# Two chained cross-attention layers on one core: the start of the kernel reordered, x rounded on another engine

## The chip, the cores and the metric

One Trainium2 chip, one core. The time is the device time of one execution in microseconds (us), and the number that counts is the median of the runs. Per core there are TensorE (PE, with its weight loads shown as PEld), VectorE (DVE), ScalarE (ACT), GpSimd (POOL), and SyncE (SP), which here only issues DMAs. The engines run independently and wait for one another through semaphores.

## The reference, cut to what matters

Two sequences of 2048 rows of 512 channels attend to 77 context rows each: first a single-head layer, then one with 16 heads.

```python
# layer 0 (one head, width 512)
q = x @ Wq.T + bq;  k = ctx @ Wk.T + bk;  v = ctx @ Wv.T + bv
s = where(mask == 0, -1e9, q @ k.T)
x = softmax(s) @ v + x
# layer 1 (16 heads, width 32 each)
Q = x @ W1q.T + b1q;  K = ctx @ W1k.T + b1k;  V = ctx @ W1v.T + b1v
o = concat_heads(softmax(Q @ K.T / sqrt(32)) @ V) @ W1o.T + b1o
y = o + x;  out = (y - mean(y)) / sqrt(var(y) + 1e-5) * gamma + beta
```

## The kernel before, in words

**Folded weights.** The layer-0 scores come from a folded matrix `a0` (W0q applied to the keys `k0T`) and an offset `c0`. Layer 0's output is never formed. Its values are folded instead: `u` = v0 @ W1q.T (function `fold`, one for each of the 2 batch entries) is added into the layer-1 queries, and `v0_a`/`v0_b` = v0 + b1o is added into the output.

**Split precision.** Operands of the large products are split into a rounded part and a remainder (`x_h`/`x_l`, `wq_h`/`wq_l`, `wo_h`/`wo_l`, `ct_h`/`ct_l`, `u` and `v0`). Each product takes three matmuls per 128 channels. The 77-row parts of `u`, `v0` and of layer 0's probabilities `p0` are stacked with their remainders by small DMAs inside the on-chip memory (`stack_weights`, `stack_probs`, both through `move`, L267), so that they need two matmuls instead of three. A query group is then 14 matmuls: 8 with `x_h`, 4 with `x_l`, and 2 with the stacks `u` and `p0`.

**Units.** The 4096 rows are 8 blocks of 512. A block has 4 units (`g` = 0 to 3), one for each group of 4 heads, so 32 units in all (`k` = 0 to 31). Unit k on TensorE: scores of unit k (64 small matmuls), and then, interleaved by hand, four transpose groups of the probabilities of unit k-1, the 14 query matmuls of unit k+1, a part of the output product of the block before (56 matmuls per block), and `context` of unit k-1. In g=0 `layer0` of the next block follows, and in g=3 `transpose0` of its probabilities. In units 0 to 3 there is no earlier block, so no output product.

**The other engines in a unit.** DVE takes four row maxima (`largest`), ACT four groups of exponentials (`exps`), DVE four sums and reciprocals (`inverse_sums`), and POOL scales (`scale_probs`). ACT empties each transpose group (`leave_pt`), rounds the context result (`round_ct`), and writes `q` (`round_q`). ACT also rounds the next block's x, two chunks in a unit with g=1 and two with g=2 (`round_x`, L450). POOL forms the remainder (`x_rest`, L323). Every engine works strictly in the order written. There are 8 PSUM banks, bank 0 for the queries, 1 to 4 scores, 5 transposes (`ps_t`), 6 context (`ps_pv`), 7 output (`ps_out`).

**The start.** SP queues these loads in order: ctx, w0k and w0q in halves, x of block 0, w0v, w1q, then w1k, w1v and w1o into buffers as they come free. ACT's own queue loads the column biases, the mask, `bo_sb` and `rows_sb`; the last two are one row of HBM broadcast to 128 partitions. TensorE does k0T, a0, c0, v0T, layer0 of block 0, k1T, the v0 rows (`to_rows`), transpose0, fold(0), 12 query matmuls, half of v1T, the last 2 query matmuls, the other half of v1T, and enters unit 0. `fold(1)` is in unit 1. DVE does layer 0's softmax first and forms `wq_l` (L656) after it.

Of the kernel before, what the change touches and what calls it, by code (L numbers as in the profile page):

```python
# [5 lines left out]
F32 = mybir.dt.float32  # L6
# [10 lines left out]
P = 128  # L17
# [22 lines left out]
STEPS = UNITS + 2  # L40
LAST = BLOCKS - 1


def xattn_kernel(nc, xT, x, mask, ctxT, w0k, w0q, w0v, w1q, w1k, w1v, w1o, cols, rows, out):
# [7 lines left out]
    with ExitStack() as ctx:  # L52
# [7 lines left out]
        with ExitStack() as prep:  # L60
# [22 lines left out]

        wq_h = sb("wq_h", [P, CH, DIM], F32R)
# [137 lines left out]
        def _(sp):  # L222
# [7 lines left out]
            sp.dma_start(raw2[:], w1q.rearrange("(c p) e -> p c e", p=P)).then_inc(ld_w1q, 16)  # L230
            sp.wait_ge(mm_k0T, 2)
# [3 lines left out]
            sp.wait_ge(mm_v0T, 2)  # L235
            sp.dma_start(raw3[:], w1o.rearrange("(c p) e -> p c e", p=P)).then_inc(ld_w1o, 16)
# [80 lines left out]
        def _(pool):  # L317
# [80 lines left out]
            pool.wait_ge(ld_rows, 16)  # L398
# [29 lines left out]
        def _(act):  # L428
            act.dma_start(cols_sb[:].rearrange("p a c -> p (a c)"), cols).then_inc(ld_cols, 16)
            act.dma_start(mask_sb[:].rearrange("p t k -> p (t k)"), mask[0, 0]).then_inc(ld_mask, 16)  # L430
            flat = rows.rearrange("(o n) -> o n", o=1)
            act.dma_start(bo_sb[:], flat[:, 2 * DIM:3 * DIM].to_broadcast([P, DIM])).then_inc(ld_bo, 16)
            act.dma_start(rows_sb[:].rearrange("p a d -> p (a d)"),
                          flat[:, 0:2 * DIM].to_broadcast([P, 2 * DIM])).then_inc(ld_rows, 16)
# [8 lines left out]
            def round_x(i, b, first, last):  # L443

                if not block_exists(i, b):
                    return
                wait(act, ld_xT, 16 * (blocks(i, b) + 1))
                wait(act, q_done, CH * blocks(i, b - 1))
                for c in range(first, last):
                    nc.scalar.activation(x_h[:, b % 2, c], x_raw[:, c], ACT.Copy).then_inc(xh_ready, 1)  # L450
# [28 lines left out]
            act.wait_ge(bk1_ready, 1)  # L479
            leave(bank[1:3], mm_k1T, k1T, bk1_scaled, k1T_ready, scale=SCALE)  # L480
# [9 lines left out]
            leave(bank[5:7], mm_v1T, v1T, cols_sb[:, 5], v1T_ready, first=2, last=CH)  # L490
# [31 lines left out]
            def step(i, k):  # L522
# [624 lines left out]
```

## Time and profile before

| | before |
|---|---|
| median of 3 runs | 425.58 us (423.49 to 426.01) |
| profiled execution: time / span of the core | 424.65 us / 422.9 us |
| PE busy | 392.4 us (93%) |
| ACT busy | 278.4 us (66%) |
| DVE busy | 276.3 us (65%) |
| POOL busy | 225.3 us (53%) |
| chain that ended last | PE 78%, DMA 7%, ACT 6% of the span |
| mean granted TensorE clock | 0.985 |

The span runs from the first to the last instruction. The profiled execution lies 0.93 us below the median and 1.75 us above its own span. A share of 93% is a mean over a start, a long middle part and an end, which have different limits, so the stages have to be read one by one.

### The profile page before, as it was taken

What the parts mean: (1) busy time and instruction counts of PE and PEld (TensorE: products, weight loads), DVE (VectorE), ACT (ScalarE), POOL (GpSimd) and SP (SyncE); (2) the same over time, 40 slices, a digit from 0 to 9 for tenths busy, and PEclk for the clock granted to TensorE, in tenths of its full rate; (3) what the DMA queues carried; (4) which work ended last, traced back from release to release, by engine and by line L of the source; (5) the groups of instructions that cost most, each with busy time, mean ns of one, the idle gap of its engine ahead of it and who ended that gap; (6) DMA issues with size and microseconds to landing.
All of it is one profiled execution on the core that took longest, in us unless ns stands there. A gap on an engine that the chain in (4) does not pass through costs nothing.

```text
span 422.9 us, 12177 instructions
## 1 busy us (share of the span) xinstructions
PE 392.4 (93%) x4968; PEld 297.5 (70%) x4968; DVE 276.3 (65%) x675; ACT 278.4 (66%) x811; POOL 225.3 (53%) x249
## 2 busy tenths in 40 slices
PE   2999988799999999999999999999999999899990
PEld 2996755577777777787777776878777776677570
DVE  0145466558766887678766876697678876557656
ACT  0433778677768865896688667877688658756720
POOL 0400357234437754785477553775377637812866
PEclk9999999899999999999999999999999999899997
DMA  8993103300024300521042204230243002240012
GB/s 254 399 327 125 48 2 131 131 16 4 1 57 167 116 11 19 184 97 52 1 170 84 95 2 138 86 126 2 72 150 127 2 21 81 81 151 2 34 66 99
DMA packets 19230, 39.44 MB, mean 93 GB/s; under 512 B 1865, under 2 KB 5449, under 8 KB 18151
## 3 DMA queue, kind: packets, MB, share of 16 engines
q1 hardware_dynamic: 18599, 37.72, 25.9%
q10 hardware_dynamic: 576, 0.96, 0.8%
q8 instruction: 39, 0.64, 0.6%
q14 instruction: 16, 0.13, 0.1%
HBM read 26.49 MB, written 8.39 MB: 82 GB/s over the span
## 4 chain that ended last, share of the span: by engine, by line
PE 78%; DMA 7%; ACT 6%; SPq 2%; POOL 2%; DVE 2%; issue 1%; POOLq 0%
PE ps_q L912 20%; PE ps_out L977 19%; PE ps_t L937 12%; PE ps_s L926 7%; PE ps_pv L952 7%; DMA p_b<-p_l 5%; PE ps_out L873 4%; PE ps_s L849 3%; ACT prob L497 2%; SPq L267 2%; DMA raw<-in_w0k 2%; ACT pt L506 1%; PE ps_pv L886 1%; PE ps_pv L849 1%; PE ps_s L994 1%
## 5 line engine op out<-in xcount | busy, mean ns | idle before, releaser
L344 POOL TENSOR_TENSOR prob<-prob,rc 128x308 f32<-128x308 f32 x128 | 91.1, 718 | 156.5 <-DVE rc L691 156.0
L497 ACT ACTIVATE prob<-ps_s,mx 128x77 f32<-128x77 f32 x512 | 120.7, 327 | 0.7 <-DVE mx L682 0.7
L506 ACT ACTIVATE pt<-ps_t 77x512 f32<-77x512 f32 x128 | 76.2, 595 | 53.1 <-PE ps_t L937 52.5
L689 DVE TENSOR_REDUCE sm<-prob 128x4 f32<-128x308 f32 x128 | 59.4, 464 | 37.8 <-ACT prob L497 37.7
L937 PE MATMUL ps_t<-ident,prob 128*77 128x128 f32 x512 | 79.7, 279 | 3.3 <-ACT pt L506 3.3
L682 DVE TENSOR_REDUCE mx<-ps_s 128x4 f32<-128x308 f32 x128 | 54.8, 471 | 36.9 <-PE ps_s L926 36.9
L937 PEld LDWEIGHTS ps_t<-ident,prob 128*77 128x77 f32 x512 | 62.1, 148 | 21.8 <-issue 5.5
L912 PE MATMUL ps_q<-x_h,wq_h 128*128 128x512 f32 x128 | 54.8, 428 | 0.0
L912 PE MATMUL ps_q<-x_h,wq_l 128*128 128x512 f32 x128 | 54.0, 422 | 0.0
L323 POOL TENSOR_TENSOR x_l<-x_raw,x_h 128x512 fp32r<-128x512 f32 x32 | 41.1, 1287 | 21.2 <-ACT x_h L450 21.2
L926 PEld LDWEIGHTS ps_s<-k1T,q 32*64 32x64 f32 x2048 | 25.9, 131 | 28.9 <-issue 16.4
L977 PE MATMUL ps_out<-wo_h,ct_h 128*128 128x512 f32 x112 | 44.9, 401 | 0.0
L977 PE MATMUL ps_out<-wo_h,ct_l 128*128 128x512 f32 x112 | 44.7, 399 | 0.0
L977 PE MATMUL ps_out<-wo_l,ct_h 128*128 128x512 f32 x112 | 44.7, 399 | 0.0
L512 ACT ACTIVATE ct_h<-ps_pv 128x512 fp32r<-128x512 f32 x32 | 19.2, 599 | 38.6 <-PE ps_pv L952 38.5
L912 PE MATMUL ps_q<-x_l,wq_h 128*128 128x512 f32 x128 | 42.2, 413 | 0.0
L360 POOL TENSOR_TENSOR y<-y,rows_sb 128x512 f32<-128x512 f32 x28 | 36.0, 1285 | 8.7 <-ACT y L519 8.7
L362 POOL TENSOR_TENSOR y<-y,rows_sb 128x512 f32<-128x512 f32 x28 | 36.0, 1287 | 2.2
L952 PE MATMUL ps_pv<-pt,v 77*32 77x512 f32 x256 | 34.1, 602 | 1.1 <-ACT pt L506 1.0
L926 PE MATMUL ps_s<-k1T,q 32*64 32x77 f32 x2048 | 31.3, 240 | 2.9 <-ACT q L468 1.8
L912 PEld LDWEIGHTS ps_q<-x_h,wq_h 128*128 128x128 f32 x128 | 25.1, 196 | 3.4 <-issue 0.3
L912 PEld LDWEIGHTS ps_q<-x_h,wq_l 128*128 128x128 f32 x128 | 24.8, 194 | 3.4 <-issue 0.2
(115 smaller groups left out, 603.4 us busy)
## 6 DMA issues: line engine op xcount, KB each, us to landing
x_raw<-in_xT SPq DMA_DIRECT2D x8, 1024.0 KB, 6.5
y<-in_x SPq DMA_DIRECT2D x28, 256.0 KB, 2.7
out<-y SPq DMA_DIRECT2D x28, 256.0 KB, 2.0
p_b<-p_a SPq DMA_DIRECT2D x8, 154.0 KB
mask_sb<-in_mask SPq DMA_DIRECT2D x7, 154.0 KB, 5.4
raw<-in_w0k SPq DMA_DIRECT2D x2, 512.0 KB, 7.5
raw<-in_w0q SPq DMA_DIRECT2D x2, 512.0 KB, 10.0
raw<-in_w0v SPq DMA_DIRECT2D x1, 1024.0 KB, 12.3
```

Source lines behind the costliest of these rows:

```text
L323: nc.gpsimd.tensor_tensor(x_l[:, b % 2, c], x_raw[:, c], f32(x_h[:, b % 2, c]), ALU.subtract).then_inc(xl_ready, 1)
L344: nc.gpsimd.tensor_tensor(ap, ap, wide(rc[:, k % 2, h], KEYS), ALU.mult).then_inc(prob_done, 1)
L360: nc.gpsimd.tensor_tensor(y[:, t], y[:, t], rows_sb[:, 0], ALU.mult).then_inc(gamma_done, 1)
L497: e = nc.scalar.activation(prob[:, k % 2, h, t], ps_s[:, h, t * KEYS:(t + 1) * KEYS], ACT.Exp, bias=mx[:, k % 2, h, t:t + 1])
L506: nc.scalar.activation(pt[:, h], ps_t[0:KEYS, :], ACT.Copy).then_inc(pt_ready, 1)
L682: nc.vector.reduce_max(mx[:, k % 2, h], ps_s[:, h, 0:TILES * KEYS].rearrange("p (t k) -> p t k", k=KEYS), AX_X, negate=True).then_inc(max_ ...
L689: nc.vector.reduce_sum(sm[:, k % 2, h], prob[:, k % 2, h], AX_X).then_inc(sum_done, 1)
L912: mm = nc.tensor.matmul(ps_q[:], w, v, start=(m == 0), stop=(m == QUERY - 1))
L926: mm = nc.tensor.matmul(ps_s[r:r + P // 2, h, t * KEYS:(t + 1) * KEYS], q[rows_of, k % 2, t * P + r:t * P + r + P // 2], k1T[rows_of, g, b ...
L937: mm = nc.tensor.transpose(ps_t[0:KEYS, t * P:(t + 1) * P], prob[:, k % 2, h, t], ident[:])
L952: mm = nc.tensor.matmul(ps_pv[rows_of, :], v1[:, b % 2, own], pt[:, h], start=True, stop=True)
L977: mm = nc.tensor.matmul(ps_out[:], w, v, start=(m == 0), stop=(m == OUTPUT - 1))
```

## The change

It does eight things.

1. Eighteen identity transposes (`WARM`) run on TensorE as soon as the identity exists, before the first load has landed.
2. ACT's queue keeps only the column biases. The mask moves to SP's queue behind w1q. `bo_sb` and `rows_sb` move to SP's queue behind the stacks, w1o and the x of block 1.
3. The w1o load moves behind the stacks of `p0` and `u` of the first batch entry.
4. ACT rounds w1q before it empties v0T. DVE forms `wq_l` before layer 0's softmax.
5. TensorE's start has layer0 before v0T, then 6 query matmuls, transpose0, fold(0), 6 more, k1T, and the last 2. v1T moves to unit 0, behind the scores, and its rows to that unit's end. wo is rounded by ACT in unit 0.
6. fold(1) moves from unit 1 to unit 2.
7. The value rows of layer 0 are made in unit 3 through `ps_out`, one batch entry at a time. TensorE waits for DVE to have read the first before it writes the second. Their stacks are SP's last step before its loop. The x load of block 2 goes in front of the `p0` stacks of block 1.
8. From block 1 on, x is rounded on DVE, behind the third sum of the units with g=1 and g=2. In g=1 ACT's exponentials and transposes follow the order of the other units.

```diff
             sp.dma_start(raw2[:], w1q.rearrange("(c p) e -> p c e", p=P)).then_inc(ld_w1q, 16)
+            sp.dma_start(mask_sb[:].rearrange("p t k -> p (t k)"), mask[0, 0]).then_inc(ld_mask, 16)
             sp.wait_ge(mm_k0T, 2)
             sp.dma_start(raw0[:], w1k.rearrange("(c p) e -> p c e", p=P)).then_inc(ld_w1k, 16)
             sp.wait_ge(mm_a0, 2)
             sp.dma_start(raw1[:], w1v.rearrange("(c p) e -> p c e", p=P)).then_inc(ld_w1v, 16)
-            sp.wait_ge(mm_v0T, 2)
-            sp.dma_start(raw3[:], w1o.rearrange("(c p) e -> p c e", p=P)).then_inc(ld_w1o, 16)
...
-            next_inputs(0, 0)
             stack_probs(0, 0)
             stack_weights(u_a, u_b, slice(0, 1), u_stacked[0], u_h_ready, u_ready, 1)
-            stack_weights(v0_a, v0_b, slice(0, BATCH), v0_stacked, v0_h_ready, v0_ready, BATCH)
-
+            sp.dma_start(raw3[:], w1o.rearrange("(c p) e -> p c e", p=P)).then_inc(ld_w1o, 16)
+            next_inputs(0, 0)
+            flat = rows.rearrange("(o n) -> o n", o=1)
+            sp.dma_start(bo_sb[:], flat[:, 2 * DIM:3 * DIM].to_broadcast([P, DIM])).then_inc(ld_bo, 16)
+            sp.dma_start(rows_sb[:].rearrange("p a d -> p (a d)"),
+                         flat[:, 0:2 * DIM].to_broadcast([P, 2 * DIM])).then_inc(ld_rows, 16)
             stack_weights(u_a, u_b, slice(1, 2), u_stacked[1], u_h_ready, u_ready, 2)
             sp.wait_ge(mm_u, BATCH)
             sp.wait_ge(wq_ready, CH)
             for t in range(TILES):
                 load_rows(0, 0, t)
+            next_inputs(0, 1)
             stack_probs(0, 1)
-            next_inputs(0, 1)
+            stack_weights(v0_a, v0_b, slice(0, BATCH), v0_stacked, v0_h_ready, v0_ready, BATCH)
...
@@ -427,11 +432,6 @@
         @block.scalar
         def _(act):
             act.dma_start(cols_sb[:].rearrange("p a c -> p (a c)"), cols).then_inc(ld_cols, 16)
-            act.dma_start(mask_sb[:].rearrange("p t k -> p (t k)"), mask[0, 0]).then_inc(ld_mask, 16)
-            flat = rows.rearrange("(o n) -> o n", o=1)
-            act.dma_start(bo_sb[:], flat[:, 2 * DIM:3 * DIM].to_broadcast([P, DIM])).then_inc(ld_bo, 16)
-            act.dma_start(rows_sb[:].rearrange("p a d -> p (a d)"),
-                          flat[:, 0:2 * DIM].to_broadcast([P, 2 * DIM])).then_inc(ld_rows, 16)
...
             act.wait_ge(ld_cols, 16)
             leave(bank[1:3], mm_k0T, k0T, cols_sb[:, 1], k0T_ready)
-            round_x(0, 0, 0, CH)
-            leave(bank[5:7], mm_v0T, v0T, cols_sb[:, 2], v0T_ready)
-            exp0(0, 0)
+            round_first_x()
             act.wait_ge(ld_w1q, 16)
             for c in range(CH):
                 nc.scalar.activation(wq_h[:, c], raw2[:, c], ACT.Copy).then_inc(wq_h_ready, 1)
-            act.wait_ge(bk1_ready, 1)
-            leave(bank[1:3], mm_k1T, k1T, bk1_scaled, k1T_ready, scale=SCALE)
+            leave(bank[5:7], mm_v0T, v0T, cols_sb[:, 2], v0T_ready, first=0, last=2)
+            exp0(0, 0)
+            leave(bank[5:7], mm_v0T, v0T, cols_sb[:, 2], v0T_ready, first=2, last=CH)
             round_p0(0, 0)
             def round_u(b):
                 act.wait_ge(mm_u, b + 1)
                 nc.scalar.activation(u_a[0:KEYS, b], bank[5 + 2 * b][0:KEYS, :], ACT.Copy).then_inc(u_h_ready, 1)
+            def round_wo(first, last):
+                act.wait_ge(ld_w1o, 16)
+                for c in range(first, last):
+                    nc.scalar.activation(wo_h[:, c], raw3[:, c], ACT.Copy).then_inc(wo_h_ready, 1)
+
             round_u(0)
-            leave(bank[5:7], mm_v1T, v1T, cols_sb[:, 5], v1T_ready, first=0, last=2)
+            act.wait_ge(bk1_ready, 1)
+            leave(bank[1:3], mm_k1T, k1T, bk1_scaled, k1T_ready, scale=SCALE)
             round_q(0, 0)
...
                 exps(i, k, 1)
+                if k == 0:
+                    leave(bank[5:7], mm_v1T, v1T, cols_sb[:, 5], v1T_ready, first=0, last=2)
+                leave_pt(i, k - 1, 2)
+                exps(i, k, 2)
+                if k == 0:
+                    leave(bank[5:7], mm_v1T, v1T, cols_sb[:, 5], v1T_ready, first=2, last=CH)
+                if g == 3:
+                    normalise(i, b - 1, 0)
+                leave_pt(i, k - 1, 3)
...
-                    round_x(i, b + 1, 0, 1)
-                    exps(i, k, 3)
-                    leave_pt(i, k - 1, 2)
-                    round_x(i, b + 1, 1, 2)
-                    leave_pt(i, k - 1, 3)
                     exp0(i, b + 1)
-                else:
-                    leave_pt(i, k - 1, 2)
-                    exps(i, k, 2)
...
+                    normalise(i, b - 2, 2)
+                if k == 0:
+                    round_wo(0, 3)
+                if k == 2:
                     round_u(1)
                 round_q(i, k + 1)
                 if g == 0:
                     normalise(i, b - 2, 3)
-                if type(i) is int and k == 0:
-                    act.wait_ge(ld_w1o, 16)
-                    for c in range(CH):
-                        nc.scalar.activation(wo_h[:, c], raw3[:, c], ACT.Copy).then_inc(wo_h_ready, 1)
+                if k == 0:
+                    for v in range(BATCH):
+                        act.wait_ge(mm_v1, v + 1)
+                        nc.scalar.activation(v1[:, v], bank[5 + v][0:KEYS, :], ACT.Copy).then_inc(v1_ready, 1)
+                    round_wo(3, CH)
...
         def _(dve):
+            def round_x(i, b, first, last):
+
+                if not block_exists(i, b):
+                    return
+                wait(dve, ld_xT, 16 * (blocks(i, b) + 1))
+                wait(dve, q_done, CH * blocks(i, b - 1))
+                for c in range(first, last):
+                    nc.vector.tensor_copy(x_h[:, b % 2, c], x_raw[:, c]).then_inc(xh_ready, 1)
+
...
             dve.wait_ge(c0_ready, 1)
+            def wq_rest(c):
+                dve.wait_ge(wq_h_ready, c + 1)
+                nc.vector.tensor_tensor(wq_l[:, c], raw2[:, c], f32(wq_h[:, c]), ALU.subtract).then_inc(wq_ready, 1)
+
+            for c in range(CH):
+                wq_rest(c)
             layer0_leave(0, 0)
             layer0_mask(0, 0)
             layer0_select(0, 0)
             layer0_shift(0, 0)
             layer0_probs(0, 0)
...
             def u_rest(b):
                 dve.wait_ge(u_h_ready, b + 1)
-                if b == 1:
-                    dve.wait_ge(v0_stacked, 48)
                 nc.vector.tensor_tensor(rest[:, b], bank[5 + 2 * b][0:KEYS, :], f32(u_a[0:KEYS, b]), ALU.subtract).then_inc(u_ready, 1)
             p0_rest(0, 0)
             u_rest(0)
-            dve.wait_ge(ld_bo, 16)
-            for b in range(BATCH):
-                dve.wait_ge(mm_v0, b + 1)
-                nc.vector.tensor_tensor(v0o[:, b], bank[3 + b][0:KEYS, :], bo_sb[0:KEYS], ALU.add).then_inc(v0o_ready, 1)
-            for v in range(BATCH):
+
+            def v0_leave(v):
+                dve.wait_ge(ld_bo, 16)
+                dve.wait_ge(mm_v0, v + 1)
+                nc.vector.tensor_tensor(v0o[:, v], ps_out[0:KEYS, :], bo_sb[0:KEYS], ALU.add).then_inc(v0o_ready, 1)
                 dve.wait_ge(v0o_ready, v + 1)
                 nc.vector.tensor_copy(v0_a[0:KEYS, v], v0o[:, v]).then_inc(v0_h_ready, 1)
...
                 inverse_sums(i, k, 2)
+                if g == 1:
+                    round_x(i, b + 1, 0, 2)
                 if g == 2:
+                    round_x(i, b + 1, 2, CH)
                     variance(i, b - 1, 0)
+                if k == 3:
+                    v0_leave(0)
                 inverse_sums(i, k, 3)
-                if type(i) is int and k == 1:
+                if k == 2:
                     u_rest(1)
+                if k == 3:
+                    v0_leave(1)
+                    v0_rest(0)
+                    v0_rest(1)
...
+            pe.wait_ge(ident_ready, 1)
+            for _ in range(WARM):
+                nc.tensor.transpose(ps_out[:, 0:P], ident[:], ident[:])
             pe.wait_ge(ld_ctx, 16)
             project(bank[1:3], raw0, ctxT_sb, mm_k0T, ld_w0k)
             pe.wait_ge(k0T_ready, CH)
@@ -1023,15 +1040,10 @@
             for c in range(CH):
                 mm = nc.tensor.matmul(ps_out[:, 0:BATCH * KEYS], bq0_wide[:, c], k0T[:, c], start=(c == 0), stop=(c == CH - 1))
             mm.then_inc(mm_c0, 1)
-            project(bank[5:7], raw3, ctxT_sb, mm_v0T, [ld_w0v, ld_w0v])
             pe.wait_ge(a0_ready, 2)
             pe.wait_ge(c0_ready, 1)
             layer0(0, 0)
-            project(bank[1:3], raw0, ctxT_sb, mm_k1T, [ld_w1k, ld_w1k])
-            pe.wait_ge(v0T_ready, CH)
-            pe.wait_ge(ident_ready, 1)
...
+            pe.wait_ge(wq_ready, 3)
+            query(0, 0, 0, 6)
+            pe.wait_ge(ident_ready, 1)
+            pe.wait_ge(v0T_ready, CH)
             transpose0(0, 0)
             fold(0, 0, CH)
             pe.wait_ge(wq_ready, CH)
-            query(0, 0, 0, 3 * CH)
-            pe.wait_ge(u_ready, 1)
-            pe.wait_ge(p0l_ready, 1)
-            project(bank[5:7], raw1, ctxT_sb, mm_v1T, [ld_w1v, ld_w1v], 0, 2)
-            pe.wait_ge(u_stacked[0], 48)
+            query(0, 0, 6, 3 * CH)
+            project(bank[1:3], raw0, ctxT_sb, mm_k1T, [ld_w1k, ld_w1k])
             query(0, 0, 3 * CH, QUERY)
-            project(bank[5:7], raw1, ctxT_sb, mm_v1T, [ld_w1v, ld_w1v], 2, CH)
             pe.wait_ge(k1T_ready, CH)
-            pe.wait_ge(v0o_ready, BATCH)
             def step(i, k):
                 g, b = k % CH, k // CH
...
                     pe.wait_ge(wo_ready, CH)
                 scores(i, k)
-                if type(i) is int and k == 0:
-                    pe.wait_ge(v1T_ready, CH)
-                    to_rows(bank[5:7], v1T, mm_v1)
-                if type(i) is int and k == 1:
+                if k == 0:
+                    pe.wait_ge(u_ready, 1)
+                    pe.wait_ge(p0l_ready, 1)
+                    project(bank[5:7], raw1, ctxT_sb, mm_v1T, [ld_w1v, ld_w1v])
+                if k == 1:
                     pe.wait_ge(v1_ready, BATCH)
...
                 query(i, k + 1, 0, 5)
                 transposes(i, k - 1, 1)
-                if type(i) is int and k == 1:
+                if k == 2:
                     pe.wait_ge(add0_done, 2)
                     fold(1, 0, 2)
+                if k == 3:
+                    pe.wait_ge(u_ready, 2)
+                    to_rows(ps_out, v0T, 0, mm_v0)
...
                     query(i, k + 1, 5, 10)
                 transposes(i, k - 1, 3)
-                if type(i) is int and k == 1:
+                if k == 0:
+                    pe.wait_ge(v1T_ready, CH)
+                    for v in range(BATCH):
+                        to_rows(bank[5 + v], v1T, v, mm_v1)
+                if k == 2:
                     fold(1, 2, CH)
+                if k == 3:
+                    pe.wait_ge(v0o_ready, 1)
+                    to_rows(ps_out, v0T, 1, mm_v0)
                 if g == 0:
                     layer0(i, b + 1)
```

## Rows read from the trace of the kernel before

**Rows 1.** Windows of units 0 to 3 and block 3: length, PE, PEld, DVE, ACT, POOL busy, PEclk, DMA, GB/s

```profile
43.77:51.22 7.45, 7.45 (x222) 6.34 (x225) 4.15 (x12) 6.69 (x24) 2.85 (x5) 1.00 0.15 49
51.22:64.19 12.97, 10.99 (x118) 6.43 (x121) 7.59 (x21) 9.42 (x28) 8.19 (x9) 1.00 0.01 2
64.19:73.19 9.00, 7.32 (x104) 5.13 (x103) 5.90 (x15) 7.93 (x25) 6.15 (x7) 1.00 0.46 153
73.19:85.03 11.84, 9.68 (x114) 6.70 (x116) 5.44 (x14) 7.39 (x23) 3.89 (x6) 0.86 0.37 127
129.31:174.07 44.76, 44.59 (x605) 33.55 (x606) 33.89 (x83) 33.31 (x98) 28.01 (x32) 1.00 0.25 83
```

**Rows 2.** Chain that ended last, to 90 us: start, us, what held it

```profile
1.24 6.43 DMA raw<-in_w0k
...
7.80 5.86 PE ps_s L849 x32
...
14.40 4.47 PE ps_s L849 x32
...
19.92 2.10 PE ps_t L849 x16
...
24.12 2.27 PE ps_out L873 x128
...
32.11 3.45 PE ps_t L1039 x8
...
37.77 3.11 DMA u_b<-rest
...
57.91 0.52 ACT x_h L450
...
65.67 1.16 PE ps_q L912 x5
...
69.30 0.84 ACT prob L497 x4
...
79.16 4.09 DMA p_b<-p_l
```

**Rows 3.** DMA queues from 5 to 9 us: packets, MB, share of 16 engines

```profile
q10 hardware_dynamic: 267, 0.74, 62.5%
q1 hardware_dynamic: 405, 0.40, 30.0%
```

**Rows 4.** DMA queue of SP from 4 to 5 us

```profile
q1 hardware_dynamic: 369, 0.38, 107.2%
```

**Rows 5.** The page's DMA issues: KB each, median us to landing

```profile
raw<-in_w1q SPq DMA_DIRECT2D x1, 1024.0 KB, 13.6
```

**Rows 6.** Timeline of the start: start, duration, engine, line, operation, idle before

```profile
7.47 2.05 SPq L230 DMA_DIRECT2D raw<-in_w1q  x1
...
26.54 0.48 DVE L587 TENSOR_TENSOR m<-ps_out,c 128x308 f32<-128x308 f32 x1 [6.26 <-PE ps_out L873]
...
26.93 0.31 DVE L596 TENSOR_SCALAR n<-mask_sb 128x308 f32<-128x308 int32 x1
...
29.76 2.17 ACT L478 ACTIVATE wq_h<-raw 128x512 fp32r<-128x512 f32 x4
...
30.61 0.48 DVE L630 TENSOR_TENSOR m<-m,stat 128x308 f32<-128x308 f32 x1
...
31.01 2.49 DVE L656 TENSOR_TENSOR wq_l<-raw,wq_h 128x512 fp32r<-128x512 f32 x4
...
38.01 0.75 DVE L671 CAST v_a<-v0o 77x512 fp32r<-77x512 f32 x2
```

**Rows 7.** Timeline of DVE in block 3, from 138 to 176 us

```profile
141.93 0.90 DVE L596 TENSOR_SCALAR n<-mask_sb 128x308 f32<-128x308 int32 x1
...
163.61 0.86 DVE L682 TENSOR_REDUCE mx<-ps_s 128x4 f32<-128x308 f32 x2 [1.19 <-PE ps_s L926]
```

**Rows 8.** Waits of PEld, 85 to 400 us: total us, times, longest

```profile
PEld ps_q L912 <- DMA p_b<-p_l: 2.4, 5, 0.5
```

More of the change, by code:

```diff
@@ L40 @@
 STEPS = UNITS + 2
+WARM = 18
 LAST = BLOCKS - 1
@@ L64, in xattn_kernel @@
             v1T = sb("v1T", [P, CH, BATCH * KEYS], F32, prep)
-            rest = sb("rest", [KEYS, BATCH, DIM], F32R, prep)
+            k0T = sb("k0T", [P, CH, BATCH * KEYS], F32, prep)
+            bq0_wide = sb("bq0_wide", [P, CH, P], F32, prep)
             v0T = sb("v0T", [P, CH, BATCH * KEYS], F32, prep)
             v0o = sb("v0o", [KEYS, BATCH, DIM], F32, prep)
-            k0T = sb("k0T", [P, CH, BATCH * KEYS], F32, prep)
             raw0 = sb("raw0", [P, CH, DIM], F32, prep)
-            bq0_wide = sb("bq0_wide", [P, CH, P], F32, prep)
-            bo_sb = sb("bo_sb", [P, DIM], F32, prep)
             before_y = 4 * CH * BLOCK + KC * BLOCK + 2 * TILES * GCOLS
-            taken = 3 * CH * DIM + 2 * BATCH * DIM + 4 * CH * BATCH * KEYS + CH * P + DIM
+            taken = 3 * CH * DIM + BATCH * DIM + 4 * CH * BATCH * KEYS + CH * P
             sb("unused", [P, before_y - taken], F32, prep)
@@ L81, in xattn_kernel @@
         y = sb("y", [P, TILES, DIM])
+        rest = sb("rest", [KEYS, BATCH, DIM], F32R)
+        bo_sb = sb("bo_sb", [P, DIM])
         wq_h = sb("wq_h", [P, CH, DIM], F32R)
@@ L441, in leave, with round_first_x @@
                     nc.scalar.activation(to[:, c], src, ACT.Identity, bias=bias[:, c:c + 1], scale=scale).then_inc(ready, 1)
[L443 to L450, printed above, removed]
+            def round_first_x():
+                act.wait_ge(ld_xT, 16)
+                for c in range(CH):
+                    nc.scalar.activation(x_h[:, 0, c], x_raw[:, c], ACT.Copy).then_inc(xh_ready, 1)
             def exp0(i, b):
@@ L648, in _ @@
             dve.wait_ge(c0_ready, 1)
+            def wq_rest(c):
+                dve.wait_ge(wq_h_ready, c + 1)
+                nc.vector.tensor_tensor(wq_l[:, c], raw2[:, c], f32(wq_h[:, c]), ALU.subtract).then_inc(wq_ready, 1)
+            for c in range(CH):
+                wq_rest(c)
             layer0_leave(0, 0)
@@ L653, in _ @@
             layer0_probs(0, 0)
-            for c in range(CH):
-                dve.wait_ge(wq_h_ready, c + 1)
-                nc.vector.tensor_tensor(wq_l[:, c], raw2[:, c], f32(wq_h[:, c]), ALU.subtract).then_inc(wq_ready, 1)
             def u_rest(b):
                 dve.wait_ge(u_h_ready, b + 1)
-                if b == 1:
-                    dve.wait_ge(v0_stacked, 48)
                 nc.vector.tensor_tensor(rest[:, b], bank[5 + 2 * b][0:KEYS, :], f32(u_a[0:KEYS, b]), ALU.subtract).then_inc(u_ready, 1)
@@ L853, in project, with to_rows @@
                         mm.then_inc(made, 1)
-            def to_rows(banks, src, made):
-                for b in range(BATCH):
-                    for e in range(CH):
-                        mm = nc.tensor.transpose(banks[b][0:KEYS, e * P:(e + 1) * P],
-                                                 src[:, e, b * KEYS:(b + 1) * KEYS], ident[:])
-                    mm.then_inc(made, 1)
+            def to_rows(to, src, b, made):
+                for e in range(CH):
+                    mm = nc.tensor.transpose(to[0:KEYS, e * P:(e + 1) * P], src[:, e, b * KEYS:(b + 1) * KEYS], ident[:])
+                mm.then_inc(made, 1)
             def layer0(i, b):
@@ L910, in query @@
                             wait(pe, p0_stacked, 48 * (blocks(i, b) + 1))
+                            if b < BATCH:
+                                wait(pe, u_stacked[b], 48)
                         w, v = ((u_a[:, b % 2, own], p0_a[:, b % 2]), (u_b[:, b % 2, own], p0_b[:, b % 2]))[m - 3 * CH]
@@ L1029, in _ @@
             layer0(0, 0)
-            project(bank[1:3], raw0, ctxT_sb, mm_k1T, [ld_w1k, ld_w1k])
-            pe.wait_ge(v0T_ready, CH)
-            pe.wait_ge(ident_ready, 1)
-            to_rows(bank[3:5], v0T, mm_v0)
-            pe.wait_ge(ld_w1q, 16)
+            project(bank[5:7], raw3, ctxT_sb, mm_v0T, [ld_w0v, ld_w0v])
             def fold(b, first, last):
@@ L1063, in part @@
                         output(i, b - 1, OUT_AT[g][n], OUT_AT[g][n + 1])
-                if type(i) is int and k == CH - 1:
-                    pe.wait_ge(u_stacked[1], 48)
                 if type(i) is int and k == CH + 1:
```

34 lines of the change are left out of this document (10 added, 24 removed).

## Prediction

> **What bounds the kernel now.** I read the windows first, then the chain of work that ended last, then the queues and the timeline of the start.
>
> From unit 4 on TensorE is the bound: block 3 holds 44.59 us of PE work in 44.76 us [rows 1]. The change takes no matmul out of these blocks, so what it can win is won before unit 4, which starts at 85.03. In units 0 to 3 there is no output product, and PE is busy for 7.45 of 7.45, 10.99 of 12.97, 7.32 of 9.00 and 9.68 of 11.84 us [rows 1]: unit 0 is PE's, units 1 and 2 are mostly ACT's, and unit 3 has waits and a clock of 0.86.
>
> Up to unit 0 the chain runs through the loads and then through PE almost without a break. PE starts at 7.80, when the first half of w0k lands (1.24 + 6.43 = 7.67) [rows 2]. The reader should see two things there. The first 32 projection matmuls take 5.86 us and the same 32 of a0 take 4.47, a difference of 1.4 us although the granted clock is shown as full in both: the first ones run slower. And from 5 to 9 us the two broadcast loads of ACT's queue move 0.74 MB while SP's queue, with everything that the start needs, moves 0.40 MB [rows 3]; in the microsecond before, it moved 0.38 MB by itself [rows 4].
>
> **Part 1, the loads come earlier.** SP's queue could have moved 4 x 0.38 = 1.52 MB in those 4 us and moved 0.40 [rows 3, 4]; the missing 1.12 MB are 2.9 us. The mask's 0.16 MB add 0.4 to 0.5 us, since it now queues behind w1q. I take 3.4 us. Bounds: only the 0.74 MB of bytes, 1.9 us; and 5.5 MB (ctx and five loads) at 0.38 from 2.2 us on, which puts w1q at 16.7, 4.4 us earlier. w1q landed at 7.47 + 13.6 = 21.1 [rows 5, 6], and now lands at 17.7. For w0k, nearer to the front, ctx and half of w0k (0.83 MB) end near 5.0 instead of 7.7. bo_sb and rows_sb come after the x of block 1 and land, an estimate, near 45 us; their first readers are in units 3 and 5.
>
> **Part 2, eighteen transposes in front.** They start near 1.5 us. The projection's 4.47 / 32 = 0.14 us [rows 2] prices them at 2.5 us, a slow rate of twice that at 5.0, so they end between 4.0 and 6.5 against w0k at 5.0. I take a start of k0T at 5.4 and leave open whether k0T takes 4.5 or 5.9. The Trainium skill, TensorE: Matmul & The Clock Gate, Part 4, says that transposes do not count as busy for the clock gate; by that k0T would still take 5.9, otherwise 4.5. No row here shows transposes alone in front of matmuls. Part 3 shows that the whole 1.4 us hardly matter, since another chain ends later.
>
> **Part 3, up to unit 0.** PE: k0T from 5.4 to 9.9 or 11.3; its second half is emptied in 0.7; a0 and c0 take 19.92 - 14.40 = 5.5 [rows 2], to 16.1 or 17.5; 0.5 for the copy of c0; layer0 2.27, to 18.9 or 20.3; v0T 2 x 2.10, to 23.1 or 24.5; six query matmuls at 0.23 [rows 2], to 24.5 or 25.9. The other chain: w1q at 17.7, ACT's first rounding chunk (2.17 / 4) to 18.3, DVE's `wq_l` 2.49 to 20.8, and only behind it layer 0's softmax, which took from 26.54 to 31.09 [rows 6], so 4.55, to 25.4. The moved `wq_l` is thus on the path; it was hidden behind the softmax. Both meet at transpose0 near 25.4: 0.45 for it, fold(0) 3.45 [rows 2], six query matmuls 1.4, k1T 4.2, the last two 0.5, to 35.4. The stacks of `u` took from 35.56 to 40.88 behind the fold, 5.3 us [rows 2]; now from 29.3 to 34.6, hidden by k1T's end at 34.9. w1o is queued behind them, so they meet no big load. Then ACT empties k1T and writes q, and scores start at 36.5, against 43.77 [rows 1]: **7.3 us earlier.**
>
> **Part 4, units 0 to 3.**
> - Unit 0 takes over v1T, 4.2, on an engine that has no idle time there: 7.45 + 4.2 = 11.65. Its rows were in the unit before, and ACT's extra pieces (v1T 1.3, wo 2.2 and v1 1.2) add to 4.0 of exponentials and q, under PE's sum.
> - Unit 1 loses fold(1), 3.45, and two roundings on ACT. It then resembles unit 2 of before: 9.00 less 2 x 0.52 for x [rows 1, 2], plus 0.45 for exp0 and handovers: 8.7, against 12.97.
> - Unit 2 takes the fold: 7.32 + 3.45 = 10.8 of PE work less overlaps: 10.6, against 9.00.
> - Unit 3 gains the v0 rows, 0.9, and a wait. PE may not write the second half of `ps_out` until DVE has added b_o to the first, and DVE's add is queued behind the third sum, which waits for the third exponentials (0.85 a group [rows 2]), near 8.5 us into the unit; the add ends at 9.2. PE is through its other work at 7.4 and stands, with the last six query matmuls, context and the next scores queued behind. From 9.2: rows 0.4, two matmuls, then the `p0` stacks. They landed 10.1 us into the unit before (79.16 + 4.09 [rows 2]); now 2.3 MB of y rows, x and mask stand in front of them, 6 us at 0.38 from about 3 us on, so 9.5 to 10.5. Then 0.5, context 1.0. That is 11.8, and I add 0.7 for a lower clock behind the stand: 12.5, against 11.84. Its bounds are 11.3 and 15.
> - The v0 stacks are ready to be issued near 1 us into unit 4 and are wanted at its end, 9 us later: nothing.
>
> Sum: 11.65 + 8.7 + 10.6 + 12.5 = 43.45 against 41.26, **2.2 us longer.**
>
> **Part 5, from unit 4 on.** ACT loses four roundings of x in a block; PE waits for none of them, so nothing is won. DVE gains four copies. The nearest row is the cast of `v_a`, 0.375 each with POOL idle [rows 6], so 1.5 us in a block on an engine with 33.9 of 44.8 us busy [rows 1]. In g=2 two copies stand ahead of the next unit's maxima, where DVE waited 1.19 us for PE [rows 7]; 0.75 fits. The same kind of operation, L596, took 0.31 us with POOL idle and 0.90 in block 3 with POOL at work [rows 6, 7]. That fits the Trainium skill, SBUF — State Buffer, section Who interferes with whom, by which a copy or a tensor_scalar in a two-port mode and a GpSimd operation exclude each other for a whole instruction. In g=2, though, POOL waits for the very copy, so I price this part at nothing and keep the other case as a rival. `largest` feeds exp, then `round_p0`, then the stacks, for which PE already waits up to 0.5 us [rows 8]: that chain has no slack of its own.
>
> **Sum.** -7.3 + 2.2 = -5.1. On the profiled execution's own 424.65 us that is 419.6; from the median of 425.58, which is 0.9 above it, 420.5. I predict 420.0. One per cent, 4.3 us, is about what a measurement of this kernel tells from no change, so faster begins below 421.3 and slower above 429.8.
>
> **Rivals.**
> 1. *Less is won.* The loads shift by 1.9 instead of 3.4 (+1.5), unit 3's stand and the stacks behind 2.3 MB cost 2 us more, or the clock falls for longer there (the 0.86 row). For it: three chains meet in unit 3 and I laid them out without gaps. Against it: the rate in rows 3 and 4. 420.0 + 3.5 = 423.5. Chance 0.30.
> 2. *More is won.* w1q lands at 16.7, so PE's own chain sets transpose0 at 24.5 (-0.9), and unit 3 runs at 11.3 (-1.2), since its exponentials start earlier without ACT's roundings: 417.9. Chance 0.13.
> 3. *Slower: the copies queue behind POOL in every block.* Place: g=2, in front of `largest` of g=3, where the `p0` stack chain starts. If each copy takes 0.375 plus a POOL operation of 1.3, two take 3.3, less the 1.19 of slack: 2.1 us in each of six blocks, 12.7 in all, so 432.7. At 1.0 us a copy the loss is 0.8 a block and the gain of 5.1 is gone; at 1.8 us a copy it passes 429.8. For it: L596's growth. Against it: POOL's order, and rows 1 leave DVE 10 us a block. Chance 0.10.
> 4. *The change doesn't do what it says:* SP's queue stays slow without the broadcasts (HBM or the small packets, not ACT's queue, set the rate of rows 3). Then w1q lands at 21, and unit 0 starts 3.3 us later: 423.3. Chance 0.04.
>
> **How the numbers follow.** The forecast, 418.5 to 421.8, has 0.43. Range 416.5 to 425: it leaves out rival 3 and the ends of 1 and 2. Faster by over 1%: 0.8 of 0.43, 0.13, and 0.2 of 0.30: 0.55. Slower by over 1%: most of rival 3, 0.09. The rest, 0.36, is within 1%.
>
> **What the changed profile would show.** Part 1: the queue table from 5 to 9 us with SP alone near 0.38 MB/us, and w1q's landing near 17.7. Part 2: the time of the first 32 matmuls. Part 3: DVE's softmax starting when `wq_l` ends, near 20.8, and scores at 36.5. Part 4: units of 11.6, 8.7, 10.6 and 12.5, with PE standing before L859's second group of v0 rows. Part 5: PE busy over 99% of block 3 in 44.8 us, and copies near 0.4 us. I would be wrong if DVE's copies grow past 1 us, if the `p0` stacks come late in unit 3, or if TensorE's clock falls in units 1 to 3, where its gaps are.

## The result, and the profile after

The changed kernel takes 431.82 us (430.38 to 433.16) against 424.90 for the kernel before (a fourth run beside the three above): 1.0183 times as long, with a 95% interval of 1.0146 to 1.0221. The forecast was 420.0. Its profiled execution took 430.87 us, with a span of 429.0 against 422.9.

First the windows of units 0 to 4 and of block 3 in the changed kernel (length; busy time of PE, PEld, DVE, ACT, POOL; granted clock; DMA share; GB/s). They answer to [rows 1].

```profile
41.73:53.42 11.69, 11.69 (x247) 10.66 (x247) 4.15 (x12) 8.58 (x27) 4.04 (x5) 1.00 0.50 199
53.42:62.84 9.42, 7.57 (x107) 5.22 (x102) 7.66 (x18) 6.72 (x23) 3.82 (x5) 1.00 0.01 3
62.84:73.33 10.49, 10.49 (x111) 6.36 (x111) 8.25 (x22) 7.49 (x23) 9.89 (x10) 1.00 0.01 2
73.33:89.45 16.12, 10.59 (x118) 6.59 (x115) 8.59 (x20) 7.63 (x23) 4.15 (x6) 0.88 0.63 201
89.45:101.15 11.70, 10.79 (x235) 8.43 (x231) 5.32 (x14) 6.92 (x22) 2.80 (x4) 0.87 0.08 26
136.42:181.08 44.66, 44.44 (x600) 33.50 (x597) 35.10 (x87) 31.32 (x94) 28.28 (x31) 1.00 0.25 81
```

The middle is untouched: block 3 takes 44.66 us against 44.69 (129.31 to 174.00 before), with DVE 1.3 us busier and ACT 2 us less. Nearly all that is missing against the forecast lies in three places: unit 0 starts 5.2 us late, unit 3 takes 3.6 us more and unit 4 takes 2.5 us more. This table is worked out from where each unit's scores start.

| us | before | forecast | after |
|---|---|---|---|
| unit 0 starts | 43.7 | 36.5 | 41.7 |
| unit 0 | 7.5 | 11.65 | 11.7 |
| unit 1 | 13.0 | 8.7 | 9.4 |
| unit 2 | 9.1 | 10.6 | 10.5 |
| unit 3 | 11.8 | 12.5 | 16.1 |
| unit 4 | 9.2 | 9.2 | 11.7 |
| unit 5 to the end | 328.7 | 328.7 | 327.9 |

Next the chain that ended last, in the changed kernel (start, us, what held it). It answers to [rows 2].

```profile
1.24 4.71 DMA raw<-in_w0k
...
6.09 4.98 PE ps_s L863 x32
...
17.79 2.35 PE ps_out L885 x128
20.13 0.72 PE ps_t L863 x4
20.86 2.88 issue
23.74 3.03 PE ps_t L863 x12
26.77 2.58 PE ps_pv L863 x16
...
79.08 7.31 DMA p_b<-p_l
...
86.44 1.22 PE ps_q L926 x2
87.65 1.87 PE ps_pv L966 x8
89.52 1.35 PE ps_s L940 x63
```

The reader should see two stands. At 20.86 PE stops for 2.88 us in the middle of v0T, held by nothing that the profile names ("issue"). The remaining 28 matmuls then take 5.6 us, where 3.7 were due, so the whole projection takes 9.2 us instead of 4.2; the granted clock is 0.70 from 23.74 to 29.35 us. And the `p0` stacks of block 1 land 7.31 us after their last issue, where it was 4.09 [rows 2]. Behind this stand too everything is slow: the context takes 1.87 us instead of 1.0, and the granted clock of units 3 and 4 is 0.88 and 0.87.

### The profile page after: what moved, and what is told of

It reads as the page before. It is cut to its first block, busy times and chain, and to the rows that moved or that the text cites. A ratio compares the mean times of both kernels' runs of the same rounds, so it can differ in the third digit from the quotient of the medians.

```text
span 429.0 us, 12203 instructions
## 1 busy us (share of the span) xinstructions
PE 397.7 (93%) x4986; PEld 301.0 (70%) x4986; DVE 288.0 (67%) x703; ACT 265.1 (62%) x783; POOL 228.3 (53%) x249
## 4 chain that ended last, share of the span: by engine, by line
PE 79%; DMA 7%; ACT 5%; SPq 3%; issue 2%; POOL 2%; DVE 1%; POOLq 0%
PE ps_q L926 20%; PE ps_out L991 19%; PE ps_t L951 13%; PE ps_s L940 7%; PE ps_pv L966 7%; DMA p_b<-p_l 6%; PE ps_out L885 4%; PE ps_s L863 3%; SPq L267 2%; PE ps_t L863 1%; ACT prob L498 1%; DMA raw<-in_w0k 1%; PE ps_pv L863 1%; ACT pt L507 1%; PE ps_pv L898 1%
## 5 line engine op out<-in xcount | busy, mean ns | idle before, releaser
L327 POOL TENSOR_TENSOR x_l<-x_raw,x_h 128x512 fp32r<-128x512 f32 x32 | 44.5, 1396 | 23.1 <-ACT x_h L447 13.4
L926 PE MATMUL ps_q<-x_h,wq_h 128*128 128x512 f32 x128 | 53.9, 421 | 0.0
L513 ACT ACTIVATE ct_h<-ps_pv 128x512 fp32r<-128x512 f32 x32 | 19.2, 600 | 40.6 <-PE ps_pv L966 40.6
L926 PEld LDWEIGHTS ps_q<-x_h,wq_h 128*128 128x128 f32 x128 | 24.5, 191 | 3.2 <-issue 0.3
```

What stands on the lines that cost most here:

```text
L327: nc.gpsimd.tensor_tensor(x_l[:, b % 2, c], x_raw[:, c], f32(x_h[:, b % 2, c]), ALU.subtract).then_inc(xl_ready, 1)
L926: mm = nc.tensor.matmul(ps_q[:], w, v, start=(m == 0), stop=(m == QUERY - 1))
```

## The experiments

All are the changed kernel with one edit or several. Ratios are to the kernel before, taken beside it on the same chip.

**1. Stacks in front of the x load.**

```diff
-            next_inputs(0, 1)
             stack_probs(0, 1)
+            next_inputs(0, 1)
```

> The changed kernel, with the stacks of block 1's probabilities put back in front of the x and mask load of block 2 on SP's queue. In the changed kernel unit 3 lasts 16.1 us, PE stands 2.8 us for these stacks, and unit 4 lasts 11.7 us where it lasted 9.2 before. Theory A (the stacks queue behind 1.2 MB of x and mask): they land 4 to 5 us after the last of them is issued instead of 7.3, unit 3 shortens by 3 us, and unit 4 by 1 to 2 us because the clock no longer falls; in all 4 to 5 us less. Theory B (the 1 MB of y rows, which stands in front in both orders, holds them back): less than 1 us. Theory C (the wait for the first v0 rows sets unit 3): unit 3 stays above 15 us.

Measured: 427.26 us, ratio 1.0072 (1.0033 to 1.0112), against 1.0183 unedited. Unit 3 takes 11.80 us, unit 4 10.68. SP's queue in this kernel, in time order, and PE's first matmul behind the stacks, which names no wait:

```profile
74.94 1.86 SPq L252 DMA_DIRECT2D y<-in_x  x4
77.65 0.81 SPq L267 DMA_DIRECT2D p_b<-p_a  x1
78.51 0.72 SPq L267 DMA_DIRECT2D p_a<-p_l  x1
79.27 0.80 SPq L267 DMA_DIRECT2D p_b<-p_l  x1
80.18 0.56 SPq L245 DMA_DIRECT2D x_raw<-in_xT  x1
...
83.81 0.49 PE L926 MATMUL ps_q<-p_a,u_a 128*128 128x512 f32 x1
```

In the changed kernel the x load was issued at 76.56, just in front of the stacks, and this matmul ran at 86.44. Theory A holds: units 3 and 4 shorten by 16.12 + 11.70 - 11.80 - 10.68 = 5.3 us. What unit 4 still has above its 9.2 is mostly 1.07 us of "issue" inside its layer0. The start kept its stand, 2.72 us.

**2. v0T in front of layer0 again.**

```diff
+            project(bank[5:7], raw3, ctxT_sb, mm_v0T, [ld_w0v, ld_w0v])
             pe.wait_ge(a0_ready, 2)
             pe.wait_ge(c0_ready, 1)
             layer0(0, 0)
-            project(bank[5:7], raw3, ctxT_sb, mm_v0T, [ld_w0v, ld_w0v])
```

> The changed kernel, with TensorE's v0T projection back in front of layer0 of block 0. In the changed kernel PE stands 2.9 us inside v0T, 20.9 to 23.7 us, with nothing released, and then runs slowly. Theory A (layer0 runs through its 128 small matmuls in 2.3 us, faster than the instructions behind them are fetched): the stand goes or falls under 1 us, and scores of unit 0 start near 38.5 us instead of 41.7. Theory B (the stand belongs to the time, not to the order: the queues are full of loads then): a stand of 2 to 3 us is seen between 19 and 25 us whatever stands there, and scores start near 41.

Measured: 433.25 us (427.30 to 434.83). The four runs lie too far apart for a ratio, so only the rows of the start are used. The stand is gone, as theory A had it, but unit 0 starts at 41.12 all the same. The chain shows why:

```profile
17.12 2.10 PE ps_t L863 x16
19.22 2.10 PE ps_pv L863 x16
21.32 2.32 PE ps_out L885 x128
23.66 0.48 DVE m L589
...
28.37 1.11 PE ps_pv L898 x4
29.47 4.39 PE ps_t L1051 x8
```

v0T takes its 4.2 us. Layer0 ends 3.5 us later, layer 0's softmax starts 1.3 us later and is now bare: PE waits 3.2 us for it, and the fold behind that wait takes 4.39 us instead of 3.45. The order avoids one stand and uncovers another wait, so its expected 38.5 us failed.

**3. The same order, but the queue empty.**

```diff
-            sp.wait_ge(mm_k0T, 2)
+            sp.wait_ge(l0_done, 1)
             sp.dma_start(raw0[:], w1k.rearrange("(c p) e -> p c e", p=P)).then_inc(ld_w1k, 16)
-            sp.wait_ge(mm_a0, 2)
             sp.dma_start(raw1[:], w1v.rearrange("(c p) e -> p c e", p=P)).then_inc(ld_w1v, 16)
```

> The changed kernel, with w1k and w1v loaded only when layer0 of block 0 is done (near 20 us) instead of at 11 and 16 us, so that SP's queue is empty from about 20 us while PE runs into v0T. Theory B (the instruction fetch queues behind w1k and w1v): the stand of 2.9 us shrinks to under 1 us and scores of unit 0 start near 38.5 us. Theory A (the fetch is late whatever the queue holds, because layer0 uses instructions up too fast): the stand stays above 2 us. w1k would land near 25 us, before its use at 31.

Measured: 428.61 us, ratio 1.0108 (1.0064 to 1.0151). Unit 0 starts at 37.51, 4.2 us earlier, while units 3 and 4 stay long (16.03 and 12.25 us). Here TensorE's timeline of this kernel at the place of the stand:

```profile
19.05 0.79 PE L862 MATMUL ps_t<-ctxT_sb,raw 128*128 128x154 f32 x4
20.10 1.84 PE L862 MATMUL ps_t<-ctxT_sb,raw 128*128 128x154 f32 x12 [0.26 <-issue]
```

And in the changed kernel:

```profile
20.06 0.79 PE L863 MATMUL ps_t<-ctxT_sb,raw 128*128 128x154 f32 x4
23.74 0.53 PE L863 MATMUL ps_t<-ctxT_sb,raw 128*128 128x154 f32 x2 [2.88 <-issue]
```

TensorE's instructions and their order are the same in both, and only SP's loads differ: the stand falls from 2.88 to 0.26 us. The DMA table names the packets. In the changed kernel, from 21 to 22 us, beside a full load queue:

```profile
q1 hardware_dynamic: 195, 0.40, 101.4%
q8 instruction: 1, 0.02, 5.8%
```

This is the first packet on that queue (it starts at 21.5 us). With late loads it starts at 17.9 us, where the load queue is running empty, and PE stands only 0.26 us. So a fetch of instructions came 3.6 us later while w1k and w1v were moving, or 2.7 us later if one counts from the start of layer0 (17.79 and 16.77 us), and PE, which had used up the 256 instructions of layer0 in 2.35 us, ran dry. Experiments 2 and 3 together say that the stand needs both: the burst of layer0 just in front, and the loads.

That the packet is TensorE's is inferred from the times; the table doesn't say. The times agree closely, though. Nine kernels stop at this place, and in each PE goes on 2.2 to 2.7 us after the packet starts: 21.5 and 23.74 in the changed kernel, 17.9 and 20.10 here, 22.5 and 25.12 in experiment 7.

The same sign stood in the kernel before, one block later, and the prediction passed over it:

```profile
48.94 2.28 PE ps_out L873 x128
...
52.05 0.99 issue
```

Here layer0 of block 1 is followed by a stand of 0.99 us, again 2.5 us behind a packet of the kind "instruction" (50.5 and 53.04), and here the DMA engines are all but idle (share 0.02). All thirteen kernels stand there for 0.55 to 0.99 us. So behind such a burst PE can stand for up to 1 us with hardly a load in flight; at the start, with the loads, it was 2.9. That the burst is the cause of the shorter stand is inferred: no run moves that layer0 away.

**4. x rounded on ACT again** (the copies on DVE removed, `round_x` back in ACT's order).

> The changed kernel, with x rounded on ACT as in the kernel before (one chunk behind the third and one behind the fourth exponentials of the units with g=1 and g=2). If the rounding on DVE costs nothing in the middle of the kernel, as forecast, the blocks from 3 on keep their 44.5 to 45.2 us, and units 1 and 2 get up to 1 us longer each: 0 to 2 us slower in all. If the copies on DVE hold up the maxima, blocks 2 to 6 get shorter by 0.3 us or more each and the kernel is 1 to 3 us faster.

Measured: 434.05 us, ratio 1.0227 (1.0182 to 1.0273). Unit 1 takes 10.40 us instead of 9.42. From unit 5 to the start of unit 31 it takes 1.7 us more, 1.5 of it in unit 29, where nothing is rounded. (Unit 29 takes 13.68 us here and 12.16 in the changed kernel, but 13.61 in the kernel before too, at a granted clock of 0.87.) The intervals of this ratio and of the changed kernel's overlap, so a gain from DVE is not shown here; experiment 8 shows it.

**5. Edits 1 and 3 together.**

> The changed kernel with two edits at once: the stacks of block 1 in front of the x load of block 2, and w1k and w1v loaded only when layer0 of block 0 is done. Theory: the two causes are separate and add up. Unit 0 starts near 37.5 us, unit 3 takes 11.8, unit 4 starts near 81.1 and takes 9.2 to 10.7; a span near 421 us and a time near 422.5, 1 to 3 us under the kernel before and 8 to 9 us under the changed kernel. Rival: with unit 0 earlier, another transfer (the u stacks behind w1k and w1v, or the y rows) takes the place, and the sum is 2 us or more short of that.

Measured: 423.09 us, ratio 0.9968 (0.9941 to 0.9995); span 420.1. Unit 0 starts at 37.74, unit 4 takes 10.06. Against the changed kernel's 1.0183 the ratio falls by 0.0215 here, by 0.0111 in experiment 1 and by 0.0075 in experiment 3: the causes add up. Unit 3 takes 13.41 instead of 11.8, since the stacks land 6.09 us after their last issue and this wait of PE is back in part:

```profile
PE ps_q L925 <- DMA p_b<-p_l: 1.4, 1, 1.4
```

**6. The same without the eighteen transposes** (`WARM = 0`).

> The same as the run before it in this set (both edits), without the eighteen identity transposes. If they raise the clock, the first 32 projection matmuls take 5.9 us again instead of about 5.0. The scores of unit 0 should still start within 0.5 us of the other run, since the chain through w1q and layer 0's softmax ends later than PE's. 36 instructions less in front also shift where PE runs out of fetched instructions: if the 1 us stand at the end of layer0 in unit 4 belongs to the position in the instruction stream, it moves or goes.

Measured: 421.85 us, ratio 0.9957 (0.9930 to 0.9984). Two lines of its chain:

```profile
5.62 7.30 PE ps_s L862 x32
...
39.16 0.94 PE ps_s L939 x45
```

k0T takes 7.30 us, against 4.56 in experiment 5 and 5.86 in the kernel before, and unit 0 starts at 39.16, 1.4 us later than with the transposes, which is more than expected. But units 3 and 4 take 12.40 and 9.22 instead of 13.41 and 10.06, and the two kernels can't be told apart. The stand at the end of layer0 in unit 4 (0.50 us in experiment 5) is gone.

**7. Mask and broadcasts back on ACT's queue** (with edits 1 and 3).

> Both edits, with the mask and the two broadcast rows back on ACT's queue at the very start. If the broadcasts hold SP's queue back, w0k and w1q land 2 to 3 us later (w0k near 7.7, w1q near 21), and unit 0 starts 2 to 2.7 us later; the rest stays. If they don't matter, unit 0 starts within 0.5 us.

Measured: 425.88 us, ratio 1.0019 (0.9988 to 1.0051), against 0.9968 without: 2.2 us of time. From 5 to 9 us SP's queue moves 0.39 MB again, against 1.31 in experiment 5. w0k lands at 7.1 us and w1q at 21.4 (5.6 and 18.6 in experiment 5), about as expected. Unit 0 starts at 41.60, 3.9 us later, which is more than the expected 2 to 2.7: k0T takes 7.43 us though the transposes ran, and PE stood 1.6 us between them and the load. (This profiled execution took 430.33 us, above the kernel's median, so of its rows only the start is used.)

**8. Rounding on ACT** (with edits 1 and 3).

> Both edits, with x rounded on ACT as before. Expected: 1 to 2 us slower than with the rounding on DVE, nearly all of it in units 1 and 2, and nothing from unit 5 on. If the rounding on DVE costs anything in the middle, blocks 2 to 6 are shorter here.

Measured: 424.98 us, ratio 1.0022 (0.9988 to 1.0057), 2.3 us above experiment 5, with intervals that overlap only at their edges. Units 1 and 2 take 10.47 and 12.04 us instead of 9.69 and 10.47. In unit 2 the granted clock is 0.86 here and 1.00 there, so its 1.6 us are a slow stretch of the clock in this one execution, and whether the rounding brought it on isn't shown. Blocks 2 to 6 take 224.4 against 223.4 us, so they aren't shorter. Nothing was expected there; 1.2 us are unit 20, which takes 10.47 us here and 9.31 in experiment 5, but 10.48 in the changed kernel with its rounding on DVE.

**9 to 11. The y rows behind the stacks.** Edits 1 and 3, and on SP's queue:

```diff
-            sp.wait_ge(mm_u, BATCH)
-            sp.wait_ge(wq_ready, CH)
-            for t in range(TILES):
-                load_rows(0, 0, t)
             stack_probs(0, 1)
             next_inputs(0, 1)
             stack_weights(v0_a, v0_b, slice(0, BATCH), v0_stacked, v0_h_ready, v0_ready, BATCH)
+            sp.wait_ge(mm_u, BATCH)
+            sp.wait_ge(wq_ready, CH)
+            for t in range(TILES):
+                load_rows(0, 0, t)
```

> The changed kernel with both edits (stacks in front of the x load, w1k and w1v late) and the four y row loads of block 0 moved behind the stacks of block 1, the x of block 2 and the stacks of v0. With both edits alone PE still stood 1.4 us in unit 3 for the stacks, which landed 6.1 us after their last issue. Theory: the y rows (1 MB) in front of them are what is left, because fold(1) in unit 2 releases them right there. Then the stacks land 4.1 to 4.5 us after the issue, the stand goes, unit 3 takes 11.8 instead of 13.4 us, unit 4 9.3 to 10; 1.5 to 2.5 us faster. Rival: the v0 rows' own wait keeps unit 3 above 13.

> The same three edits without the eighteen identity transposes. Unit 0 starts 1.4 us later (39.1 against 37.7), as in the pair without the third edit; units 3 and 4 take 11.8 and 9.3. If the transposes are worth what unit 0 shows, this is about 1 us slower than the other; if the stand for instructions at the end of layer0 in unit 4 comes from their 36 instructions, the two are equal within 0.5 us.

> The three edits, with the transposes, and w1q queued in front of w0v. Unit 0's start hangs on w1q (landed at 18.6 us), its rounding, and layer 0's softmax behind it. With w1q 2.5 us earlier, PE's own chain (layer0 at 20, v0T to 24.4, six query matmuls) sets transpose0, near 25.8 instead of 26.5: 0.5 to 0.8 us gained, no more. If w0v then lands after 20 us and PE waits for it, nothing or a loss.

Measured: 423.67 us, ratio 1.0000 (0.9963 to 1.0037); without transposes 423.28, 0.9975 (0.9942 to 1.0008); with w1q in front 424.62, 1.0005 (0.9973 to 1.0038). Unit 3 takes 11.71 us in all three, so the y rows were what was left. But the expected 1.5 to 2.5 us were not gained: it was paid back at once. TensorE in unit 4 of the first of them:

```profile
87.02 2.34 PE L884 MATMUL ps_out<-a,x_raw 128*32 128x77 f32 x127
90.79 0.23 PE L884 MATMUL ps_out<-a,x_raw 128*32 128x77 f32 x1 [1.44 <-issue]
...
92.80 1.12 PE L950 MATMUL ps_t<-ident,prob 128*77 128x128 f32 x4
```

The y rows are now issued from 83.6 to 87.4 us, the queue is busy right under layer0 (0.33 MB from 88 to 89 us), and layer0 stands 1.44 us for its last instruction (0.50 in experiment 5). Unit 5 follows at a granted clock of 0.59 (93 to 97 us) and takes 13.74 us instead of 12.16. Without transposes unit 0 starts at 38.20 instead of 37.35, and unit 4 takes 9.26 instead of 11.00. w1q in front gives nothing: PE's own chain already set transpose0 (26.28 and 26.21 us).

## Why the prediction was wrong

**Part 1, the loads: right mechanism, size too large.** SP's queue moved 1.29 MB from 5 to 9 us, not 1.52, and w1q landed at 5.51 + 13.7 = 19.2, 1.9 us earlier, not 3.4. Experiment 7 shows that the loads on ACT's queue are the cause, and that they cost 2.2 us of time. The mask had landed at 4.6 us there, so from 5 to 9 us it was the two broadcasts.

**Part 2, the transposes: they do raise the clock.** k0T took 4.98 us behind them, and 7.30 without (experiment 6); in experiment 3 the transposes themselves speed up, from one in 0.21 us to one in 0.11. Only the estimate that this hardly matters was roughly right: they were worth 1.4 and 0.85 us in unit 0's start, and nothing that could be told in the kernel's time.

**Part 3 failed, in its step "v0T 2 x 2.10, to 23.1 or 24.5".** I took the projection from its matmuls, as if PE's instructions were always there. It took from 20.1 to 29.35: 2.9 us of stand and 2.1 us of slower matmuls (granted clock 0.70). Experiment 3 removes the stand without touching TensorE's program, and unit 0 starts at 37.5, 4.2 us earlier; 0.7 of the 1.0 us by which that misses the forecast's 36.5 is w1q's landing (18.4 against 17.7). In the kernel before, v0T's 64 instructions stood between a0 and layer0, and PE didn't stop there: its packet started at 22.9 us, before layer0 began at 24.12. I had not asked what the moved block does to the fetch. In the same move ACT's exp0 stood behind the emptying of v0T, so the softmax waited with it. Unit 0's late start is 5.2 of the 11.3 us that the profiled execution lies above the forecast for it (430.87 against 419.6).

**Part 4 failed in unit 3, in its step "so 9.5 to 10.5".** The stacks landed 13.1 us into the unit. I had named the 2.3 MB in front of them, and counted their bytes at 0.38 MB/us, but from 76 to 82 us SP's queue moved only 0.30 to 0.34, and the last stack took 7.3 us from issue to landing. Moving the x load behind them removed the stand in experiment 1 and left 1.4 us of it in experiment 5, which moving the y rows cleared in 9. The wait for the v0 rows, which I had made unit 3's limit, was there (1.2 us), and with the queue clear unit 3 took 11.7 to 11.8, my sum without the clock's share. Unit 3 is 3.6 us of the 11.3.

**A term was missing: unit 4.** I let the slower clock end with unit 3. It ran on into unit 4 (0.87), which also has layer0 and its own 0.9 us for instructions: 2.5 us. Rival 1 had the loads, the stacks and the clock at 3.5 us together; no rival had the fetch.

**Right:** units 0, 1 and 2 (11.7, 9.4, 10.5 against 11.65, 8.7, 10.6), the hidden `u` stacks, and most of Part 5. Unit 1 is the loosest: its own terms, 9.00 - 1.04 + 0.45, give 8.4 and not 8.7. DVE's copies took 0.42 us in the median and 1.35 at most; block 3 kept its length; rival 3 didn't happen. Rival 4 is refuted by the 1.29 MB. Freeing ACT was worth 2.3 us in time (experiment 8), where the forecast had counted 1.0 in unit 1. The units show 0.8 to 1.0 in unit 1 (experiments 4 and 8); the 1.6 in unit 2 of experiment 8 stand beside a lower clock, so where the rest comes from is open.

**Two more sums were off, without effect on the outcome.** In rival 3 the time passes 429.8 from 1.4 us a copy on, not from 1.8: 2 x 1.4 less 1.19, in six blocks, is 9.7. And 0.8 of 0.43, 0.13 and 0.2 of 0.30 make 0.53, not 0.55.

**Open:** why the clock's share differs from run to run; why the packet came late in the changed kernel and in experiments 1 and 4, but in time in the kernel before and in experiment 2, where the load queue was as full when it came (102.9% and 104.4% of the engines in that microsecond); and what sets the length of the stand in unit 4. Its place goes with the 36 instructions of the transposes: all ten kernels that have them stand 0.50 to 1.57 us at the end of that layer0, and of the two changed ones without them experiment 6 doesn't stand and experiment 10 stands 0.49 us one step later, at the scores of unit 5.

The version of experiment 6 beats both kernels, by 0.4% the one before and by 2.2% the changed one (0.9957 and 1.0183 to the same kernel, on two chips). The forecast's 420.0 wasn't reached: the gains are there, but they are smaller than one per cent.

## What to carry to other kernels

A dense burst of small matmuls can use up instructions faster than they are fetched: here up to 1 us with idle DMA engines, and 2.7 to 2.9 us when large loads filled them. So keep big, non-urgent loads away from such a burst. Where the chain shows a long "issue" behind one, look in the DMA table for a packet of the kind "instruction" 2 to 3 us before the engine goes on. A small transfer that somebody waits for should be issued in front of the large ones on its queue, and each step that is moved (here the fold, which released the y rows) moves those loads too. A stand of TensorE can cost more than its length (2.9 us and then 2.1 of slower matmuls): price the slower matmuls behind it, into the next unit.

## What the runs showed of the hardware

- **The clock and transposes.** Without transposes the 32 matmuls of k0T took 5.86, 7.30 and 6.90 us (the kernel before, experiments 6 and 10). With eighteen fp32 transposes directly ahead of them they took 4.5 to 5.4 us wherever no load interrupted them: 4.98 in the changed kernel, 5.23 and 5.30 in experiments 2 and 9, and 4.57, 4.56 and 4.46 in experiments 3, 5 and 8. With transposes and then 1.6 us of idle they took 7.43 (experiment 7, one execution). a0's 32 take 4.47 us everywhere. Where k0T is slower than that, the spacing of its matmuls falls from 0.26 to 0.13 us at one point. In experiments 3, 5 and 8 it is 0.13 us from the second matmul on, and in experiment 3 the transposes themselves speed up, from 0.21 to 0.11 us apart near 4.6 us, when nothing else had run. The Trainium skill, TensorE: Matmul & The Clock Gate, Part 4, has it that transposes do not count as busy for the clock; these runs disagree, as far as these fp32 transposes go. The profile's granted clock reads 1.00 in all these stretches, so the start has to be read from the spacing of the matmuls.
- **Broadcast loads.** 768 KB from one row of HBM to 128 partitions held SP's queue to 0.40 MB in 4 us; without them it moved 1.29 MB. The two queues together moved 1.14 MB, so this was mostly a sharing of the same engines.
- **Instruction fetch.** It shares the DMA engines with the data. With the same order on PE, it stood 2.7 to 2.9 us in the three kernels with w1k and w1v in flight, and 0.2 to 0.7 us in the six with these loads held back. A fetch that meets nearly idle DMA engines can be late too: 0.55 to 0.99 us behind the second layer0 in all thirteen kernels.
